# Four images side by side in the partitions: 16 KB runs instead of 4 KB in a streaming masked batch norm

## The reference, cut to what matters

```python
g = v.reshape(B_, G, C_ // G, H_, W_)            # G = 32
m, s = mean(g, axis=(2, 3, 4)), var(g, axis=(2, 3, 4))
gn = (g - m) / sqrt(s + 1e-5)
x1 = gn.sum(axis=1)                              # over the 64 channels
mask = x1 != 0
var_c = masked variance of gn per channel over all 16 images
out = x + where(mask, gn / sqrt(var_c + 1e-3), gn)
```

## Time and profile before

| | |
|---|---|
| median of three runs | 1295.09 us |
| span of the profiled execution | 1293.2 us |
| bytes read and written | 268.44 MB each |
| PE, DVE, ACT, POOL busy | 57%, 62%, 63%, 41% of the span |
| DMA over the span | 416 GB/s |

### The profile page before, as it was taken

One profiled execution on the slowest core, in us unless ns is written; L12 is line 12 of the kernel. 1 busy time (PEld: TensorE's weight loads), 2 busy tenths in 40 slices (PEclk: granted clock), 3 DMA queues, 4 the chain that ended last, 5 costly groups with the idle time before them and its releaser, 6 DMA issues.

```text
span 1293.2 us, 10692 instructions
## 1 busy us (share of the span) xinstructions
PE 741.7 (57%) x2882; PEld 302.4 (23%) x2882; DVE 796.5 (62%) x1892; ACT 816.4 (63%) x950; POOL 535.1 (41%) x504
## 2 busy tenths in 40 slices
PE   0766654566545665456654566544665446654475
PEld 0222222222222222122221222212222122222232
DVE  6776666566665666655666556665566655666563
ACT  0777555775557755567655676556765567755575
POOL 0055333454334544345443444434443444533450
PEclk9988767887678876688766887667887678866788
DMA  9999999999999999999999999999999999999997
GB/s 378 415 421 420 421 421 421 422 420 420 421 421 421 420 421 421 421 421 420 421 421 421 421 421 420 421 420 421 421 421 421 420 420 421 418 421 418 420 414 281
DMA packets 135469, 537.58 MB, mean 416 GB/s; under 512 B 4336, under 2 KB 4336, under 8 KB 135408
## 3 DMA queue, kind: packets, MB, share of 16 engines
q1 hardware_dynamic: 69936, 276.83, 52.3%
q10 hardware_dynamic: 65472, 260.05, 49.0%
HBM read 268.44 MB, written 268.44 MB: 415 GB/s over the span
## 4 chain that ended last, share of the span: by engine, by line
DMA 60%; ACT 15%; PE 11%; DVE 7%; issue 5%; SPq 0%; ACTq 0%
DMA out_dram<-slots 37%; DMA slots<-in_x_dram 23%; ACT slots L346 11%; PE flush L421 6%; ACT fresh L343 4%; DVE stats L471 2%; DVE spread L454 2%; PE stay L417 1%; PE stay L418 1%; PE small_ps L386 1%; PE small_ps L396 1%; DVE dev L517 1%; PE small_ps L397 1%; ACT sums L343 0%; SPq L237 0%
## 5 line engine op out<-in xcount | busy, mean ns | idle before, releaser
L471 DVE BATCH_NORM_STATS2 stats<-slots 128x6 f32<-128x512 f32 x1024 | 631.5, 680 | 437.8 <-DMA slots<-in_x_dram 436.5
L346 ACT ACTIVATE slots<-slots,out_bias,out_scale 128x1024 f32<-128x1024 f32 x512 | 622.4, 1245 | 2.3 <-DVE out_bias L528 1.3
L325 POOL TENSOR_TENSOR sums<-fresh,sums 128x512 f32<-128x512 f32 x360 | 458.8, 1274 | 363.6 <-ACT fresh L343 363.6
L421 PE MATMUL flush<-slots,weights 128*64 128x512 f32 x1536 | 442.0, 695 | 42.2 <-ACT fresh L343 40.6
L343 ACT ACTIVATE fresh<-flush,group_bias 128x512 f32<-128x512 f32 x360 | 246.5, 685 | 51.8 <-PE flush L421 51.8
L302 POOL TENSOR_TENSOR weights<-pair_sum,group_rstd 128x256 f32<-128x256 f32 (+1 forms) x128 | 73.2, 602 | 357.5 <-DVE group_bias L508 357.5
L421 PEld LDWEIGHTS flush<-slots,weights 128*64 128x64 f32 x1536 | 131.7, 156 | 295.9 <-issue 294.3
L358 ACT ACTIVATE by_image<-by_image,eps 128x16 f32<-128x16 f32 x32 | 9.8, 307 | 242.2 <-DVE by_image L495 241.8
L417 PE MATMUL stay<-slots,weights 128*64 128x512 f32 x512 | 140.0, 606 | 0.0
L418 PE MATMUL stay<-minus_mean,weights 128*64 128x512 f32 x512 | 138.1, 593 | 0.0
L386 PE MATMUL small_ps<-spread,group_avg 128*128 128x64 f32 x64 | 21.8, 443 | 183.3 <-DVE spread L491 183.3
(11 more groups left out here) (52 smaller groups left out, 234.5 us busy)
## 6 DMA issues: line engine op xcount, KB each, us to landing
slots<-in_x_dram SPq DMA_DIRECT2D x127, 2048.0 KB, 17.7
out_dram<-slots ACTq DMA_DIRECT2D x124, 2048.0 KB, 29.9
out_dram<-slots SPq DMA_DIRECT2D x16, 512.0 KB, 5.1
slots<-in_x_dram SPq DMA_DIRECT2D x4, 512.0 KB, 13.6
```

Of the source, the lines that this page charges most:

```text
L325: pool.tensor_tensor(into, fresh[:, n % FRESH_BUFS, :], into, ALU.add).then_inc(added, 1)
L346: nc.scalar.activation(out_in_ring(u, i), image_in_ring(u, i), ACT.Identity, bias=out_bias[:, u % 2, i:i + 1], scale=out_scale[:, u % 2, i ...
L421: nc.tensor.matmul(into, weight, source, start=True, stop=True).then_inc(image_summed, 1)
L471: last = V.bn_stats(stats[:, u % 2, k * BLOCK_STATS:(k + 1) * BLOCK_STATS], source)
```

## The change

A tile now holds four images side by side in the partitions. Partition `4*r + a` of tile `t` holds elements `r*4096` to `r*4096 + 4095` of the unit's part of image `4*t + a`, with `r` from 0 to 31 and `a` from 0 to 3: one run of 16 KB in memory and in the partition. Partitions 0 to 63 are still the unit's first channel. A tile is still 2 MB, a unit still four tiles, a DMA still one tile.

What used to be per image is now per set of four images (`SETS` = 4), with each partition knowing its own image's value: those arrays are 4 columns wide instead of 16, and the folds are 4 x 16 instead of 16 x 4. `group_avg` is no longer constant; it joins only partitions with the same `p % 4`, made by two more DVE instructions at the start. POOL makes one weight set for each tile. The last tile's four loads and the last unit's 16 stores still move 512 KB each, now as chunks of 1024 columns of a set. The number of DMAs, matmuls, ACT instructions and blocks of DVE is the same.

```diff
-TILE_IMAGES = 4
+SIDE = 4
+TILE_CHUNKS = 4
-    FOLDS = 2 * BLOCKS
+    SETS = B // SIDE
+    SET_N = SIDE * N
+    FOLDS = 2 * BLOCKS * SIDE
-    x_rows, out_rows = (t.rearrange("b c w h -> b (c w h)").rearrange("b (u p n) -> u p b n", u=UNITS, p=P) for t in (x, out))
+    x_rows, out_rows = (t.rearrange("b c w h -> b (c w h)").rearrange("(t a) (u r n) -> u t r a n", a=SIDE, u=UNITS, n=SET_N)
+                        for t in (x, out))
+        def tile_in_ring(j):
+            at = j % RING * TILE_N
+            return slots[:, at:at + TILE_N]
         def in_dram(rows, j):
-            i = j % UNIT_TILES * TILE_IMAGES
-            return rows[j // UNIT_TILES, :, i:i + TILE_IMAGES, :]
+            t, part = divmod(j % UNIT_TILES, SET_TILES)
+            return rows[j // UNIT_TILES, t, :, :, part * TILE_N:(part + 1) * TILE_N]
+        def chunk_in_dram(rows, u, i):
+            at = i % SIDE * N
+            return rows[u, set_of(i), :, :, at:at + N]
-                    sp.dma_start(in_ring(j), in_dram(x_rows, j)).then_inc(loaded[j % RING], 16)
+                    sp.dma_start(tile_in_ring(j), in_dram(x_rows, j)).then_inc(loaded[j % RING], 16)
-                        sp.dma_start(in_ring(j)[:, i, :], in_dram(x_rows, j)[:, i, :]).then_inc(last_loaded[i], 16)
+                        sp.dma_start(in_ring(j)[:, i, :], chunk_in_dram(x_rows, LAST, B - TILE_CHUNKS + i)).then_inc(last_loaded[i], 16)
-                sp.dma_start(out_rows[LAST, :, i, :], out_in_ring(LAST, i)).then_inc(last_stored, 16)
+                sp.dma_start(chunk_in_dram(out_rows, LAST, i), out_in_ring(LAST, i)).then_inc(last_stored, 16)
-                act.dma_start(in_dram(out_rows, j), in_ring(j)).then_inc(stored[j % RING], 16)
+                act.dma_start(in_dram(out_rows, j), tile_in_ring(j)).then_inc(stored[j % RING], 16)
-            def weigh(u, first, n, matrix):
-                at = u * B + first
-                return pool.tensor_tensor(weights[:, u % 2, first:first + n, :], matrix.unsqueeze(1).to_broadcast([P, n, ROWS]),
-                                          group_rstd[:, at:at + n].unsqueeze(2).to_broadcast([P, n, ROWS]), ALU.mult)
+            def weigh(u, t, sign, matrix):
+                at = u * SETS + t
+                return pool.tensor_tensor(weights[:, u % 2, sign, t, :], matrix,
+                                          group_rstd[:, at:at + 1].to_broadcast([P, ROWS]), ALU.mult)
                     if u < LAST:
-                        weigh(u, part[0], EVERY, pair_sum[:, :]).then_inc(weights_ready, 1)
+                        weigh(u, t, 0, pair_sum[:, :]).then_inc(weights_ready, 1)
                     else:
-                        weigh(u, part[0], EVERY - 1, minus_pair_sum[:, :]).then_inc(weights_ready, 1)
-                        weigh(u, part[-1], 1, pair_sum[:, :]).then_inc(weights_ready, 1)
+                        weigh(u, t, 1, minus_pair_sum[:, :]).then_inc(weights_ready, 1)
+                        weigh(u, t, 0, pair_sum[:, :]).then_inc(weights_ready, 1)
+            V.tensor_reduce(side[:, :], unit_matrix.rearrange("p (j a) -> p a j", a=SIDE), AX_X, ALU.add).then_inc(matrices_ready, 1)
+            dve.wait_ge(matrices_ready, 3)
+            V.tensor_scalar(group_avg[:, :].rearrange("p (j a) -> p j a", a=SIDE), side[:, :].unsqueeze(1).to_broadcast([P, P // SIDE, SIDE]),
+                            1.0 / (HALF_UNIT * IMAGE_FOLDS), None, ALU.mult).then_inc(matrices_ready, 1)
```

More of the change, by code:

```diff
@@ L110, in norm_conv_kernel @@
         eps = sb("eps", [P, 2])
+        side = sb("side", [P, SIDE])
+        all_avg = sb("all_avg", [P, P])
         group_avg = sb("group_avg", [P, P])
@@ L137, in norm_conv_kernel @@
             by_unit[:, i, :] for i in range(10))
-        few = held[:, 7680:7680 + 3 * B + 1]
-        pad, has_pad, n_image, first_row = few[:, 0:B], few[:, B:2 * B], few[:, 2 * B:3 * B], few[:, 3 * B:3 * B + 1]
+        few = held[:, 7680:7680 + 4 * SETS + 1]
+        pad, has_pad, n_image, n_set = (few[:, i * SETS:(i + 1) * SETS] for i in range(4))
+        first_row = few[:, 4 * SETS:4 * SETS + 1]
+        n_by_side = held[:, 7800:7800 + B].rearrange("p (a t) -> p a t", a=SIDE)
         flush = [psum(f"flush{i}", [P, BLK]) for i in range(FLUSH_BANKS)]
@@ L166, in norm_conv_kernel @@
         flag_ready = sem("flag_ready")
-        last_loaded = [sem(f"last_loaded{i}") for i in range(TILE_IMAGES)]
+        last_loaded = [sem(f"last_loaded{i}") for i in range(TILE_CHUNKS)]
         last_stored = sem("last_stored")
@@ L255, in _, with set_in_dram, set_on_chip, load_half @@
                         sp.dma_start(into[:, :, k, :], not_zero[k * ROWS:(k + 1) * ROWS, :, :]).then_inc(mask_spread, 16)
[L257 to L261, removed]
+                def set_in_dram(rows, u, t):
+                    return rows[bass.ds(u, 1), t, :, :, :].rearrange("o r a n -> (o r) a n")
+                def set_on_chip(v, t):
+                    at = t % HALF_SETS * SET_N
+                    return v[:, at:at + SET_N]
+                def load_half(u, a):
+                    for t in range(a * HALF_SETS, (a + 1) * HALF_SETS):
+                        sp.dma_start(set_on_chip(tile_x, t), set_in_dram(x_rows, u, t)).then_inc(tile_loaded, 16)
                 for sweep in range(2):
@@ L369, in _ @@
                     put_out(u, i)
-                    if u < LAST and i and i % TILE_IMAGES == 0:
-                        store(u, i // TILE_IMAGES - 1)
+                    if u < LAST and i and i % TILE_CHUNKS == 0:
+                        store(u, i // TILE_CHUNKS - 1)
                 if u < LAST:
@@ L413, in channel_sums @@
                     for k in range(BLOCKS):
-                        into, weight = bank[k * ROWS:(k + 1) * ROWS, :], weights[:, u % 2, i, :]
+                        into = bank[k * ROWS:(k + 1) * ROWS, :]
+                        weight = weights[:, u % 2, 1 if u == LAST and i in flushed else 0, t, :]
                         source = image_in_ring(u, i)[:, k * BLK:(k + 1) * BLK]
@@ L425, in _ @@
                 channel_sums(u)
-            small(UNITS * SMALLS + 1, count_ps, group_avg[:, :], n_row)
+            small(UNITS * SMALLS + 1, count_ps, all_avg[:, :], n_row)
             pe.wait_ge(flag_ready, 1)
@@ L595, in tile_g @@
                 def tile_g(sweep, u, a, k):
-                    dve.wait_ge(tile_loaded, u * (HALVES * 16) + (sweep * GENERAL_TILES + a + 1) * 16)
-                    for i in range(HALF_IMAGES):
-                        at = bass.ds(u * B + (a * HALF_IMAGES + i), 1)
-                        last = V.tensor_scalar(tile_a[:, i * N:(i + 1) * N], tile_x[:, i * N:(i + 1) * N], group_mean[:, at],
+                    dve.wait_ge(tile_loaded, u * (HALVES * HALF_MOVES) + (sweep * GENERAL_TILES + a + 1) * HALF_MOVES)
+                    for i in range(HALF_SETS):
+                        at = bass.ds(u * SETS + (a * HALF_SETS + i), 1)
+                        columns = slice(i * SET_N, (i + 1) * SET_N)
+                        last = V.tensor_scalar(tile_a[:, columns], tile_x[:, columns], group_mean[:, at],
                                                group_rstd[:, at], ALU.subtract, ALU.mult)
```

134 lines of the change are left out of this document (75 added, 59 removed).

## The result

The changed kernel takes 1276.96 us (median of 4 runs, 1276.84 to 1278.15) against 1295.06 us for the kernel before: ratio 0.9862, 95% interval 0.9849 to 0.9876. It is 18.1 us faster. The forecast was 36.2 us, from 1295.09 to 1258.9. The sign held and so did the wide range, 1247 to 1288; the forecast's own band, 1247 to 1267, did not, and the size was twice what came. The profiled execution took 1278.15 us and has a span of 1276.4 us, 16.8 us less than before.

What follows compares the result with a forecast made beforehand. The DMA engines' packet rate was taken to bound the kernel. Larger packets save 34.3 us mixed and 1.9 us on lone loads, 36.2 us off the 1293.2 us span, plus 1.9 us to the median: 1258.9 us, range 1247 to 1267.

Steps and rivals of the forecast that it cites:

- What bounds the kernel: Whole span: the DMA engines' rate limit, flat at 418 to 422 GB/s, binds; no compute engine is busy above 63%.
- The 16 KB packet: Ring loads and stores: one packet every 605.1 ns instead of four at 155.7 ns each, saving 36.2 us in all.
- The upper end that I gave for the packet: Ring loads and stores: no overlap left, 608.9 ns a packet, saving 28.9 us, so 1266.2 us.
- that packets alone don't overlap: Loads running alone at the start: 159.5 ns long and passed every 159.8 ns; mixed packets overlap by 3.8 ns.
- The ends keep 4 KB packets and save nothing, cost at nothing: The 4 loads and 16 stores of 512 KB: no saving, and their rows 16 KB apart cost nothing.
- the engine that is last is busy to the end: Kernel's end: the last of 16 DMA engines works throughout, so all its packet savings count.
- Issue: SP and ACT queues: issues stuck up to 10.4 and 4.1 us become immediate; nothing on the path.
- Set-up, weights, small operations: Start, DVE statistics and POOL weights: under 0.9 us a unit saved on DVE, all beside transfers, not counted.
- Rival 1: Ring of loads and stores takes back half the gain: 18 us saved, 1277 us, range 1267 to 1288; chance 0.15.
- Rival 2: Nothing happens: 16 KB runs are cut into 4 KB packets, or bytes are the limit; 1295 us, chance 0.06.
- Rival 3: A 16 KB data packet costs what the instruction fetch did, 0.928 us: 1908 us; any above 622.8 ns is slower; chance 0.10.
- Rival 4: Neighbouring partitions 16 MB apart in memory make engines take turns in pairs: 1195 us more, 2490 us; chance 0.04.

Runs made afterwards that it cites:

- the copies: Transfers alone, output equal to input: layout of the kernel before with 4 KB packets, 1280.72 us; new layout with 16 KB packets, 1253.05 us.

## Why the prediction was right or wrong

*What bounds the kernel*: right. A flat rate in the slices was a rate of the DMA engines, and the copies show it with no compute at all, 422 GB/s against 421.

*The 16 KB packet*: right in form, one term mis-sized. Overlap 3.8 ns forecast, 3.6 found. Bytes 149.8 ns for each 4 KB forecast, 151.3 found. The 149.8 came from one 8 KB packet of an instruction fetch, and that row was not misleading: 8 KB data packets are 309 ns long too. What failed is the step from it to 16 KB. It took the 8 KB packet less the mean of the 4 KB ones, 159.5 ns where nearly all are 159, and carried that on, while 8 KB more cost 302 ns and not 2 x 149.8. Some 2 ns of the 4.7 are that (611.1 in the copy against 608.9), 2 are the few longer packets of the full kernel, and most of the rest is the completion packets, four times as many for each data packet. A difference of 1.5 ns is nothing beside 155.7, but it is taken three times, and what the change can win is itself only the fixed part: 3 x 1.5 = 4.5 of the 17.7 ns that a 16 KB packet was to save against four of 4 KB. Over 243 DMAs it is 243 x 8 x (609.8 - 605.1) ns = 9.1 us of the 18.1 missing. The upper end that I gave for the packet, 608.9 ns and 1266.2 us, was below what came. One reading in the working is wrong: that packets alone don't overlap. 101.4% of 16 x 40 us for 16.22 MB is 163.9 ns a packet, passed on every 159.8, an overlap of 4.1 ns. What differs alone is the length of the packet. That the overlap stays at 16 KB came true, but not for the reason that I gave for my choice.

*The ends keep 4 KB packets and save nothing, cost at nothing*: wrong, and with the price of bytes this is the step that failed. I asked what those packets cost themselves and what their addresses cost. I didn't ask who stands beside them in the engines. With turns by the packet, small packets next to large ones get one part in five of an engine. The last tile landed 31.0 us after its issue, where the same four DMAs beside 4 KB stores need 14.2. Loading the tile whole gives 8.6 us back, which the same edit in the kernel before does not (0.4 us). The two steps together are 17.7 of the 18.1 us. That the engine that is last is busy to the end, so that all its savings count, failed with it: from 1240 to 1250 us the changed kernel moves 25 GB/s, so the engine that is last isn't busy to the end any more.

The rest is small terms in both directions, which I didn't take apart: the hole of 383 GB/s from 40 to 50 us, before enough stores are issued, costs 1.1 us; the fall after 900 us, 2.9 GB/s over 300 us in the version with its last tile whole, 2.0 us, of which the kernel before had 0.5 already. On the other side the slow last 7 us of the earlier trace rows are mostly gone: the changed kernel moves 258 GB/s in its last 7.2 us, not 21.

*Issue*: right. The issues of the changed kernel, duration minimum, median and maximum in ns, against the earlier trace rows:

```profile
L262 SPq DMA_DIRECT2D slots<-in_x_dram x127: 534/535/2064, 0.8 to 1197.5; - x127
L383 ACTq DMA_DIRECT2D out_dram<-slots x124: 546/547/672, 44.0 to 1230.7; - x124
```

The longest issue of SP is 2.06 us, not 10.4, and nothing follows from it. But an issue costs more by itself: a median of 535 ns on SP and 547 on ACT, not 367 and 378, for the new access pattern. That I had missed; it lies beside other work here.

*Set-up, weights, small operations*: right as long as transfers cover them. In the last unit they don't: from 1242.22 to 1248.93 us the changed kernel's chain is the statistics alone, 6.7 us, with the DMA engines nearly idle. I had counted all of it as beside the transfers.

*Rival 1*, the ring: it takes a little back late in the run, far less than the 18 us I priced it at, though 1277 us is the very number that I gave for it. The number was right by accident: slices stand at 430 GB/s with the DMA row at 9 tenths, so most of the loss wasn't the ring. *Rival 2*: no; 39,084 packets and 430 GB/s. *Rival 3*: a 16 KB data packet takes 613 ns, not the 928 of the fetch; what made that price, the destination or the queue, no run shows. *Rival 4*: no; the layout costs some 3 ns in 4.98 us, if anything. The Trainium skill's row on power-of-two pitches ("DMA: Bandwidth & Descriptors", "Latency and other measured facts") is for tiles where every partition lies one pitch from the next, so it says nothing of four neighbours 16 MB apart, and nothing of the kernel before either, whose neighbouring partitions lie 4 KB apart; I had read it as bearing on both. The same row's 214 GB/s in each direction for 16 KB tiles at a good pitch, 428 in sum, is near what came here: 430 mixed, 428 for loads alone. That my estimate from it, some 20 us, is near the 18.1 measured is luck, since half of what the forecast missed was lost at the end and not in the rate.

## What to carry to other kernels

A larger DMA packet saves only its fixed part, here 4.4 ns in 155.8. The gain is a small difference of large numbers: 1.5 ns too little for the bytes of 4 KB made it a third too large. To size it, measure the rate at the size itself, in the same ring. When packets grow, look for those that stay small: as long as the other queue is full of large ones, each small one waits for a whole large one, and at the end of a kernel that lands on the path. Make both queues' packets the same size. That the urgent queue's could be the larger follows from taking turns, but no run here tested it.

## What the runs showed of the hardware that I had not expected

- A packet costs 4.4 ns + 151.3 ns for each 4 KB with loads and stores mixed. Alone, loads cost 9.3 ns and stores 11.4 ns besides their bytes, so 4 KB streams run at 410 and 405 GB/s and the mixture at 421, while at 16 KB they run at 428, 427 and 430.
- The two queues share an engine by packets, one for one: with 4 KB loads beside 16 KB stores, 330 packets of one and 344 of the other passed in 16 us, stores landed in 11.2 us instead of 28.9 and the last piece of a tile took 35.
- Data packets are nearly all of one length: 159, 309 and 611 ns for 4, 8 and 16 KB, and the next starts 3 to 4 ns before the end.
- A completion packet is 9 ns long and costs an engine some 6 to 7 ns.
- The issue of a load went from 367 to 535 ns when its DRAM side became 32 x 4 rows instead of 128 x 4 pieces.
